# A counting sort of 50,000 edges that places the first 80 of 400 columns ahead of the other 320

## The chip, the cores and the metric

The kernel runs on one core of a Trainium2 chip. The metric is the device time of one execution in microseconds (us). A core has TensorE (PE, matrix products), VectorE (DVE, elementwise work and scans), ScalarE (ACT), GpSimd (POOL, which here writes the descriptors of indirect DMAs) and SyncE (SP, which here issues plain DMAs). They run their own instruction streams and wait for each other by semaphores.

## The reference

Four layers of a graph network on 3125 nodes of 128 features and 50,000 edges. Each layer gathers a row per edge, weighs it and sums it at the edge's target:

```python
edge_index = jnp.stack([src, dst])
h = jnp.maximum(_layernorm(x, axis=-1), 0.0)
x = x + _L0_gnn_ref(h, edge_index, edge_weight, ...)      # 3 dense layers, 2 sums over edges
h = jnp.maximum(_layernorm(x, axis=-1), 0.0)
x = x + _L1_gnn_ref(h, edge_index, edge_attr_64, ...)     # attention with 4 heads, uses edge features
h = jnp.maximum(_layernorm(x, axis=-1), 0.0)
x = x + _L2_gnn_ref(h, ..., src, dst)                     # attention with 8 heads
h = jnp.maximum(_layernorm(x, axis=-1), 0.0)
x = x + _L3_gnn_ref(h, edge_index, ...)                   # 2 gated sums over edges
```

A sum over edges is `jax.ops.segment_sum(val[:, None] * h[row], col, num_segments=N)`. The order in which the edges are summed is free, and the kernel uses that.

## The kernel before

**The sort.** Nodes are cut into 25 blocks of 128 (`NB`). Edges are sorted by the block of their target, so that later each tile of 128 edges belongs to one block and its sum is a matrix product with a one-hot matrix. The edges lie in 125 partitions (`LANES`) of 400 columns (`COLS`): `e_blk` is the block of each edge's target. Each edge has a record of 8 words (source, target within its block, weight, four edge scores) in `rec`. VectorE first counts, per partition and block, how many edges there are (line 1085), TensorE makes prefix sums of the counts over the partitions (`prefixes`, lines 775 and 776), and `base_pos[:, b]` is then the place of a partition's first edge of block b, less one.

**Placement** (lines 1103 to 1114). A loop of five rounds takes five blocks in each: five compares of `e_blk` with the block's number (`inside`, line 1105), five running sums over the columns that begin at `base_pos` (`ranks`, line 1108), and five predicated copies of the ranks to `e_pos` where the edge is in the block (line 1113), each of which waits for the one before. Lines 1116 to 1120 turn places into the rows of the DRAM table, `e_row`; line 1121 raises `s_placed`.

**Stores** (lines 442 to 452). GpSimd waits for the empty table in DRAM (`s_recinit`, filled by SyncE at line 402) and for `s_placed`, and then issues one indirect DMA for each of the 400 columns (line 449): 125 records go to the rows that `e_row` names for that column. They are in groups of 8 (`G`). Group g waits for the edge scores (`s_esc`): groups 0 to 3 for their own, all others for all 50 groups of scores; and for the stores of group g - 2 to have landed. Scores come from TensorE (transposes at line 789, products at line 799) and ScalarE (copies at lines 537 and 525), in groups of 8 columns as well, from edge features that DMAs bring in.

**Behind the stores.** SyncE waits for all stores, reads the sorted table back (line 406) and stores the node table of the first sum (lines 414 and 415). GpSimd waits for both and starts the gathers of the six sums (line 468). Meanwhile, from line 1123 on, VectorE makes tables of which tile is whose (line 1125, 25 operations), counts the edges of each node by one-hot matrices (line 1153 and 1156, multiplied by TensorE at line 822, which comes to it after the last edge product), and does the dense start of the first layer (lines 1181 to 1505). Then it waits for the sorted records (line 1269).

The order on each engine is the order of its code.

Of the kernel before, what the change touches and what calls it, by code (L numbers as in the profile page):

```python
# [8 lines left out]
ALU = mybir.AluOpType  # L9
# [3 lines left out]
P = 128  # L13
# [3 lines left out]
NB = (N + P - 1) // P  # L17
NP = NB * P
TAIL = N - (NB - 1) * P
LANES = 125  # L20
COLS = E // LANES
TILES = (E // P + NB + 15) // 16 * 16
G = 8
PAIRS = TILES // (2 * G)
GROUPS = TILES // G
SLOTS = 2 * G + 1
# [59 lines left out]
def edge_loads(eng):  # L86

    for i in range(3):
        yield i, i % 2, i // 2 + 1
    with eng.Fori(0, (COLS // 16 - 5) // 2, 1) as j:  # L90
        yield 2 * j + 3, 1, j + 2
# [21 lines left out]
def gnn_kernel(nc, x, src, dst, edge_attr, edge_weight, fc_w, fc_b, conv_w, conv_b, bn_gamma, bn_beta,  # L113
               W_node, W_edge, a_vec, Wq, bq, Wk, bk, Wv, bv, Wo, bo, Wt, bt, Wg, bg, out):
    ctx = ExitStack()
    with ctx:
# [14 lines left out]
        iota = sb("iota", [P, 512])  # L131
# [59 lines left out]
        e_w = FT[0:LANES, 2 * COLS:3 * COLS]  # L191
        e_int = FT[0:LANES, 3 * COLS:4 * COLS].bitcast(I32)
        e_blk = ACC[0:LANES, 0 * COLS:1 * COLS]
        e_sblk = ACC[0:LANES, 1 * COLS:2 * COLS]
        e_sloc = ACC[0:LANES, 2 * COLS:3 * COLS]
        e_pos = ACC[0:LANES, 3 * COLS:4 * COLS]
        e_rank = ACC[0:LANES, 4 * COLS:5 * COLS]
        row_all = ACC[:, 5 * COLS:6 * COLS].bitcast(U32)
        e_row = row_all[0:LANES, :]
        spare = sb("spare", [P, 1])  # L200
        tot = sb("tot", [LANES, NB])
        base_pos = sb("base_pos", [LANES, NB])
# [55 lines left out]
        inside = rows[0:LANES, :, :, :].rearrange("p a t f -> p (a t f)")[:, 0:5 * COLS].bitcast(I32).rearrange("p (c e) -> p c e", e=COLS)  # L258
        ranks = OH[0:LANES, :, :, :].rearrange("p a t f -> p (a t f)")[:, 0:5 * COLS].rearrange("p (c e) -> p c e", e=COLS)
# [15 lines left out]
        s_rank = sem("s_rank")  # L275
        s_masked = sem("s_masked")
        s_placed = sem("s_placed")
# [9 lines left out]
        s_esc = sem("s_esc")  # L287
# [17 lines left out]
        s_gate = sem("s_gate")  # L305
# [131 lines left out]
        @block.gpsimd  # L437
        def _(pool):
            nc.gpsimd.iota(iota_i[:, :], pattern=[[1, 512]], base=0, channel_multiplier=0).then_inc(s_iota, 1)
            nc.gpsimd.iota(lane_i[:, :], pattern=[[0, 1]], base=0, channel_multiplier=1).then_inc(s_iota, 1)  # L440

            pool.wait_ge(s_recinit, 16)
            pool.wait_ge(s_placed, 1)
            for g in range(COLS // G):
                pool.wait_ge(s_esc, g + 1 if g < 4 else COLS // G)
                if g >= 2:
                    pool.wait_ge(s_scat[(g - 2) % 3], 16 * G * ((g - 2) // 3 + 1))
                for c in range(G * g, G * g + G):
                    nc.gpsimd.indirect_dma_start(  # L449
                        rec_dram, bass.IndirectOffsetOnAxis(ap=row_all[:, c:c + 1], axis=0),  # L450
                        rec_all[:, c, :], None).then_inc(s_scat[g % 3], 16)
            pool.wait_ge(s_recl, 16)

            for k in range(len(PASSES)):
                pool.wait_ge(s_stored[k], 32)
                pool.wait_ge(s_idx, 1 if k == 0 else 2)
                idx = idx_u if k == 0 else idx_s
                for g in range(GROUPS):
                    if k in HEADS:
                        to, landed = wide[k][:, g % DEEP], s_wide[g % DEEP]  # L460
                        if g >= DEEP:
                            pool.wait_ge(s_msg, groups_before(k, ("part",)) + g - DEEP + 1)
                    else:
                        to, landed = rows[:, g % RING], s_rows[g % RING]
                        if k or g >= RING:
                            pool.wait_ge(s_part, groups_before(k, ("sum",)) + g - RING + 1)
                    for j in range(G):
                        nc.gpsimd.indirect_dma_start(  # L468
                            to[:, j, :], None, tab_dram[k],
                            bass.IndirectOffsetOnAxis(ap=idx[:, G * g + j:G * g + j + 1], axis=0)).then_inc(landed, 16)  # L470
# [551 lines left out]
        def _(dve):  # L1022
            done = [0]
            asked = [0]
            v = nc.vector

            def link(ins):
                done[0] += 1
                ins.then_inc(s_dve, 1)
                dve.wait_ge(s_dve, done[0])  # L1030
# [69 lines left out]
            link(v.memset(e_pos[:, :], 0.0))  # L1100
            link(v.memset(e_w[:, :], 0.0))

            with dve.Fori(0, NB // 5, 1) as b5:
                for c in range(5):
                    v.tensor_scalar(inside[:, c, :], e_blk[:, :], iota[0:LANES, bass.ds(5 * b5 + c, 1)], None, ALU.is_equal).then_inc(s_rank, 1)
                for c in range(5):
                    dve.wait_ge(s_rank, 15 * b5 + c + 1)
                    v.tensor_tensor_scan(ranks[:, c, :], e_w[:, :], inside[:, c, :], base_pos[:, bass.ds(5 * b5 + c, 1)],
                                         ALU.add, ALU.add).then_inc(s_rank, 1)
                for c in range(5):  # L1110
                    dve.wait_ge(s_rank, 15 * b5 + 10 + c)
                    dve.sem_inc(s_gate, 1)
                    v.copy_predicated(e_pos[:, :], inside[:, c, :], ranks[:, c, :]).then_inc(s_rank, 1)
                dve.wait_ge(s_rank, 15 * b5 + 15)

            link(v.tensor_copy(e_int[:, :], e_pos[:, :]))
            link(v.tensor_single_scalar(e_int[:, :], e_int[:, :], 7, ALU.arith_shift_right))
            link(v.tensor_copy(e_rank[:, :], e_int[:, :]))
            link(v.scalar_tensor_tensor(e_pos[:, :], e_rank[:, :], -float(P), e_pos[:, :], ALU.mult, ALU.add))
            link(v.scalar_tensor_tensor(e_row[:, :], e_pos[:, :], float(TILES), e_rank[:, :], ALU.mult, ALU.add))  # L1120
            dve.sem_inc(s_placed, 1)

            link(v.memset(tblk[:, :], 0.0))
            with dve.Fori(0, NB, 1) as b:
# [21 lines left out]
            for i in rounds(dve, COLS // G // 2):  # L1146
                for both in range(2):
                    g = 2 * i + both
                    for kind, (blk, loc) in enumerate(((e_blk[:, :], rec[:, :, R_DST]), (e_sblk[:, :], e_sloc[:, :]))):
                        buf = 2 * both + kind  # L1150
                        if there(g - 2):
                            dve.wait_ge(s_hmm, 2 * g - 3 + kind)
                        v.tensor_tensor(ohlo[:, buf * 1024:(buf + 1) * 1024].rearrange("p (g n) -> p g n", g=G),
                                        counting.unsqueeze(1).to_broadcast([LANES, G, P]),
                                        loc[:, bass.ds(G * g, G)].unsqueeze(2).to_broadcast([LANES, G, P]), ALU.is_equal).then_inc(s_rank, 1)
                        v.tensor_tensor(ohhi[:, buf, :, :], counting[:, 0:NB].unsqueeze(1).to_broadcast([LANES, G, NB]),
                                        blk[:, bass.ds(G * g, G)].unsqueeze(2).to_broadcast([LANES, G, NB]), ALU.is_equal).then_inc(s_rank, 1)
                        dve.wait_ge(s_rank, 3 * NB + 4 * g + 2 * kind + 2)
                        dve.sem_inc(s_hoh, 1)
            dve.wait_ge(s_hmm, 2 * (COLS // G))  # L1160
            for kind in range(2):
# [417 lines left out]
```

## Time and profile before

| What | Value |
|---|---|
| Median of 3 runs | 4432.37 us (4431.76 to 4432.81) |
| Profiled execution | 4432.22 us, its span 4430.4 us |
| Busy share of the span | PE 44%, VectorE 51%, ScalarE 25%, GpSimd 63% |
| GpSimd stores, line 449 | 400, 394.3 us busy, idle before them 233.4 us |
| Compares, line 1105 (125 x 400) | 25, mean 422 ns |
| Scans, line 1108 (125 x 400) | 25, mean 1027 ns |
| Predicated copies, line 1113 (125 x 400) | 25, mean 608 ns |
| Tile tables, line 1125 (128 x 416) | 25, mean 653 ns |

Times within the profile count from the start of the span. What a row calls idle is the time that an engine stood still before the instruction, with what ended it behind the arrow; "issue" means that it waited for nothing that the profile shows. An instruction's duration includes what it was held up by once it had begun.

### The profile page before, as it was taken

What the parts mean: (1) busy time and instruction counts of PE and PEld (TensorE: products, weight loads), DVE (VectorE), ACT (ScalarE), POOL (GpSimd) and SP (SyncE); (2) the same over time, 40 slices, a digit from 0 to 9 for tenths busy, and PEclk for the clock granted to TensorE, in tenths of its full rate; (3) what the DMA queues carried; (4) which work ended last, traced back from release to release, by engine and by line L of the source; (5) the groups of instructions that cost most, each with busy time, mean ns of one, the idle gap of its engine ahead of it and who ended that gap; (6) DMA issues with size and microseconds to landing.
All of it is one profiled execution on the core that took longest, in us unless ns stands there. A gap on an engine that the chain in (4) does not pass through costs nothing. (4 is left out here: it accounts for less than half of the span.)

```text
span 4430.4 us, 48122 instructions
## 1 busy us (share of the span) xinstructions
PE 1947.8 (44%) x10480; PEld 1717.4 (39%) x10507; DVE 2251.4 (51%) x5375; ACT 1094.4 (25%) x3112; POOL 2777.1 (63%) x2902
## 2 busy tenths in 40 slices
PE   7521006666433333457665445554443333433332
PEld 7411005555333333346564244544333333333332
DVE  8672027777554444346666358878523333333333
ACT  2101002222300000367775257776200000000000
POOL 0677767777467776177773077775037777177775
PEclk9997556666665556665566767777556655565555
DMA  4100012222221223133332144444011222211223
GB/s 126 37 3 3 3 38 53 53 53 52 31 57 53 52 52 48 49 76 82 79 81 31 49 129 129 129 128 85 1 38 53 53 53 52 28 52 52 53 53 51
DMA packets 145729, 254.66 MB, mean 57 GB/s; under 512 B 57658, under 2 KB 81503, under 8 KB 145300
## 3 DMA queue, kind: packets, MB, share of 16 engines
q0 software_dynamic: 99328, 193.52, 19.0%
q1 hardware_dynamic: 40058, 46.93, 3.7%
q10 hardware_dynamic: 6170, 12.57, 0.9%
q14 instruction: 145, 1.19, 0.1%
q8 instruction: 28, 0.46, 0.0%
HBM read 236.52 MB, written 16.30 MB: 57 GB/s over the span
## 5 line engine op out<-in xcount | busy, mean ns | idle before, releaser
L468 POOL DMA_INDIRECT pool<-tab_dram,tblk x1248 | 1181.8, 947 | 735.9 <-issue 379.3
L891 PE MATMUL bank<-pool 128*128 128x128 f32 x3328 | 769.6, 425 | 1522.5 <-DMA pool<-tab_dram,tblk 1037.5
L891 PEld LDWEIGHTS bank<-pool 128*128 128x128 f32 x3328 | 718.0, 327 | 1565.7 <-issue 1119.9
L468 POOL DMA_INDIRECT arena<-tab_dram,tblk x832 | 798.6, 960 | 508.0 <-DMA tab_dram<-arena 254.4
L1301 DVE TENSOR_TENSOR ACC<-ACC,bank 128x128 f32 x1664 | 476.8, 287 | 987.7 <-PE bank L891 774.5
L449 POOL DMA_INDIRECT rec_dram<-arena,ACC x400 | 394.3, 986 | 233.4 <-issue 120.1
L468 POOL DMA_INDIRECT pool<-tab_dram,arena x416 | 401.7, 966 | 141.1 <-issue 126.1
L944 PE MATMUL bank<-pool 128*128 128x136 f32 (+1 forms) x1664 | 308.6, 356 | 52.9 <-DVE pool L1374 34.2
L498 ACT ACTIVATE pool<-bank 128x512 f32<-128x512 f32 (+1 forms) x56 | 29.8, 551 | 1177.2 <-PE bank L747 1176.9
L944 PEld LDWEIGHTS bank<-pool 128*128 128x128 f32 x1664 | 292.4, 257 | 61.8 <-DVE pool L1374 37.8
L1431 DVE TENSOR_TENSOR ACC<-ACC,pool 128x132 f32 (+1 forms) x832 | 248.2, 298 | 119.2 <-DVE ACC L1431 5.8
L559 ACT ACTIVATE arena<-bank,key 128x128 bf16<-128x128 f32 x416 | 146.3, 377 | 643.8 <-PE bank L834 643.8
L618 ACT ACTIVATE pool<-iota,recS 128x128 f32<-128x128 f32 x832 | 252.8, 387 | 0.0
L920 PE MATMUL bank<-HN,pool 128*128 x832 | 155.5, 363 | 111.8 <-DVEq L1339 89.5
L920 PEld LDWEIGHTS bank<-HN,pool 128*128 128x128 f32 x832 | 143.6, 269 | 125.4 <-issue 125.4
L917 PEld LDWEIGHTS bank<-at,pool 128*128 128x128 f32 x832 | 158.9, 293 | 38.8 <-issue 38.8
L917 PE MATMUL bank<-at,pool 128*128 x832 | 158.5, 323 | 31.4 <-issue 15.7
L929 PE MATMUL bank<-ident,sg 128*128 128x128 f32 x52 | 23.1, 445 | 329.2 <-DVE lm L1363 323.2
L1197 DVE TENSOR_TENSOR pool<-bank,recS 128x1024 f32<-128x1024 f32 x104 | 127.3, 1224 | 71.4 <-issue 71.3
L1262 DVE TENSOR_SCALAR pool<-bank,arena 128x128 f32<-128x128 f32 x416 | 137.3, 401 | 39.8 <-issue 39.8
L1262 DVE TENSOR_SCALAR pool<-bank,recS 128x128 f32<-128x128 f32 x416 | 137.2, 401 | 39.9 <-issue 39.9
L929 PEld LDWEIGHTS bank<-ident,sg 128*128 128x128 f32 x52 | 9.6, 184 | 339.5 <-issue 288.9
(251 smaller groups left out, 3183.7 us busy)
## 6 DMA issues: line engine op xcount, KB each, us to landing
pool<-dst_dram SPq DMA_DIRECT2D x104, 256.0 KB, 3.5
pool<-tab_dram,tblk POOLq DMA_INDIRECT x1248
arena<-tab_dram,tblk POOLq DMA_INDIRECT x832
HN<-in_edge_attr_dram ACTq DMA_DIRECT2D x23, 500.0 KB
pool<-tab_dram,arena POOLq DMA_INDIRECT x416
rec_dram<-arena,ACC POOLq DMA_INDIRECT x400, 2.1
tab_dram<-arena SPq DMA_DIRECT2D x4, 1536.0 KB
tab_dram<-arena SPq DMA_DIRECT2D x1, 3072.0 KB
```

What stands on the lines that cost most here:

```text
L449: nc.gpsimd.indirect_dma_start(rec_dram, bass.IndirectOffsetOnAxis(ap=row_all[:, c:c + 1], axis=0), rec_all[:, c, :], None).then_inc(s_sca ...
L468: nc.gpsimd.indirect_dma_start(to[:, j, :], None, tab_dram[k], bass.IndirectOffsetOnAxis(ap=idx[:, G * g + j:G * g + j + 1], axis=0)).then ...
L559: nc.scalar.activation(signs[:, half, j, :], bank[j // 4][:, (j % 4) * P:(j % 4 + 1) * P], ACT.Sign, scale=-1.0, bias=key[:, bass.ds(G * g ...
L618: nc.scalar.activation(OHF[:, half, j, :], iota[:, 0:P], ACT.Square, scale=-1.0, bias=one[:, R_DST:R_DST + 1]).then_inc(s_osq, 1)
L891: last = nc.tensor.matmul(bank[4 + 2 * (q % 2) + j // 4][:, (j % 4) * P:(j % 4 + 1) * P], OH[:, q, j, :], rows[:, q, j, :], start=True, st ...
L917: last_ = nc.tensor.matmul(bank[4 + half][:, 4 * j:4 * j + 4], OHT[:, half, j, :], at4[:, bass.ds(vals[j], 1), :].rearrange("p b h -> p (b ...
L920: last_ = nc.tensor.matmul(bank[4 + j // 4][:, (j % 4) * P:(j % 4 + 1) * P], OHT[:, half, j, :], hn1[:, bass.ds(vals[j] * D, D)], start=Tr ...
L944: last_ = nc.tensor.matmul(bank[j // 3][:, (j % 3) * ww:(j % 3 + 1) * ww], OHF[:, half, j, :], weighed[k][:, half, j, :], start=True, stop ...
L1197: return v.tensor_tensor(to, (iota[:, 0:P] if k in HEADS else iota_p).unsqueeze(1).to_broadcast([P, G, P]), records(k)[:, bass.ds(G * g, G ...
L1262: v.tensor_scalar(OH[:, q % RING, j, :], iota_p, one[:, R_DST:R_DST + 1], one[:, R_W:R_W + 1], ALU.is_equal, ALU.mult).then_inc(s_ohw, 1)
L1301: v.tensor_tensor(acc, acc, bank[4 + 2 * (q % 2) + j // 4][:, (j % 4) * P:(j % 4 + 1) * P], ALU.add).then_inc(s_acc, 1)
L1431: v.tensor_tensor(acc, acc, own[:, j, 0:sw], ALU.add).then_inc(s_sum, 1)
```

## The change

The placement becomes a function `place(c0, c1, ranked, carry)` that works on columns c0 to c1 and is called twice, for columns 0 to 80 (`FIRST`) and 80 to 400. All instructions keep their form, with fewer columns. In the first call each round ends with a copy of the last column of `ranks` to `base_pos`, so that the second call's running sums go on from there. Each call raises `s_placed`. GpSimd begins to store after the first, with each of the first ten groups waiting for its own scores; before group 10 it waits for the second placement and for all scores. The counts on `s_rank` are moved accordingly.

```diff
+FIRST = 80
...
             for g in range(COLS // G):
-                pool.wait_ge(s_esc, g + 1 if g < 4 else COLS // G)
+                if g == FIRST // G:
+                    pool.wait_ge(s_placed, 2)
+                pool.wait_ge(s_esc, g + 1 if g < FIRST // G else COLS // G)
...
-            with dve.Fori(0, NB // 5, 1) as b5:
-                for c in range(5):
-                    v.tensor_scalar(inside[:, c, :], e_blk[:, :], iota[0:LANES, bass.ds(5 * b5 + c, 1)], None, ALU.is_equal).then_inc(s_rank, 1)
...
+            def place(c0, c1, ranked, carry):
+
+                step = 16 if carry else 15
+                with dve.Fori(0, NB // 5, 1) as b5:
+                    for c in range(5):
+                        v.tensor_scalar(inside[:, c, c0:c1], e_blk[:, c0:c1], iota[0:LANES, bass.ds(5 * b5 + c, 1)], None, ALU.is_equal).then_inc(s_rank, 1)
+                    for c in range(5):
+                        dve.wait_ge(s_rank, ranked + step * b5 + c + 1)
+                        v.tensor_tensor_scan(ranks[:, c, c0:c1], e_w[:, c0:c1], inside[:, c, c0:c1], base_pos[:, bass.ds(5 * b5 + c, 1)],
+                                             ALU.add, ALU.add).then_inc(s_rank, 1)
+                    for c in range(5):
+                        dve.wait_ge(s_rank, ranked + step * b5 + 10 + c)
+                        dve.sem_inc(s_gate, 1)
+                        v.copy_predicated(e_pos[:, c0:c1], inside[:, c, c0:c1], ranks[:, c, c0:c1]).then_inc(s_rank, 1)
+                    if carry:
+                        v.tensor_copy(base_pos[:, bass.ds(5 * b5, 5)], ranks[:, :, c1 - 1]).then_inc(s_rank, 1)
+                    dve.wait_ge(s_rank, ranked + step * b5 + step)
+
+                link(v.tensor_copy(e_int[:, c0:c1], e_pos[:, c0:c1]))
...
+                dve.sem_inc(s_placed, 1)
+
+            place(0, FIRST, 0, True)
+            place(FIRST, COLS, 16 * NB // 5, False)
```

## Rows read from the trace of the kernel before

**Rows 1.** Waits of GpSimd, 0 to 640 us: engine, line, for what, us, times, longest.

```profile
POOL rec_dram L449 <- DVEq L1121: 97.4, 1, 97.4
```

**Rows 2.** Timeline of GpSimd: start us, us, engine, line, operation, out<-in, [idle before <-releaser].

```profile
98.89 1.14 POOL L449 DMA_INDIRECT rec_dram<-arena,ACC  x1 [97.41 <-DVEq L1121]
...
139.94 0.95 POOL L449 DMA_INDIRECT rec_dram<-arena,ACC  x1 [0.30 <-issue]
155.62 0.96 POOL L449 DMA_INDIRECT rec_dram<-arena,ACC  x1 [14.72 <-ACT arena L525]
```

**Rows 3.** Timeline of all engines, 624 to 660 us.

```profile
628.20 0.96 POOL L449 DMA_INDIRECT rec_dram<-arena,ACC  x1 [0.30 <-issue]
630.34 0.35 SPq L406 DMA_DIRECT2D arena<-rec_dram  x1
...
638.39 0.53 DVE L1269 CAST arena<-arena 128x416 uint32<-128x416 f32 x1 [247.48 <-DMA arena<-rec_dram]
...
643.81 0.97 POOL L468 DMA_INDIRECT pool<-tab_dram,arena  x1 [14.65 <-DMA tab_dram<-arena]
```

**Rows 4.** Timeline of VectorE, 0 to 420 us; x5 merges five instructions.

```profile
40.04 0.21 DVE L1096 TENSOR_TENSOR_SCAN tcount<-tcount 128x25 f32<-128x25 f32 x1
...
42.24 1.78 DVE L1105 TENSOR_SCALAR pool<-ACC,iota 125x400 int32<-125x400 f32 x5 [0.26 <-DVE pool L1101]
43.93 4.81 DVE L1108 TENSOR_TENSOR_SCAN pool<-pool,base_pos 125x400 f32<-125x400 f32 x5
48.89 3.62 DVE L1113 COPY_PREDICATED ACC<-pool 125x400 f32<-125x400 int32 x5 [0.15 <-DVE pool L1108]
52.97 1.78 DVE L1105 TENSOR_SCALAR pool<-ACC,iota 125x400 int32<-125x400 f32 x5 [0.45 <-DVE ACC L1113]
...
95.58 0.37 DVE L1116 CAST pool<-ACC 125x400 int32<-125x400 f32 x1 [0.21 <-DVE ACC L1113]
...
97.40 0.58 DVE L1120 SCALAR_TENSOR_TENSOR ACC<-ACC 125x400 uint32<-125x400 f32 x1
```

**Rows 5.** Timeline of all engines, 350 to 400 us: a store beside line 1189.

```profile
351.27 3.49 DVE L1189 TENSOR_TENSOR HN<-X,stat 128x3200 f32<-128x3200 f32 x1
351.45 4.14 POOL L449 DMA_INDIRECT rec_dram<-arena,ACC  x1 [0.30 <-issue]
```

**Rows 6.** Line 402, the DMA that fills the record table: issue and landing.

```profile
L402 SPq DMA_DIRECT2D rec_dram<-recS x1: 2022/2022/2022, 25.9 to 25.9; - x1
...
DMA to landing us min/median/max: 17.1/17.1/17.1
```

**Rows 7.** Timeline of ScalarE, 20 to 60 us: the tenth copy of scores.

```profile
54.23 0.20 ACT L525 ACTIVATE arena<-bank 125x32 f32 x1 [1.00 <-PE bank L799]
```

**Rows 8.** Line 525, the copies of edge scores: duration ns, first and last start us.

```profile
L525 ACT ACTIVATE arena<-bank x50: 197/198/198, 23.3 to 155.1; 125x32 f32 x40, 125x32 f32<-125x32 f32 x10
```

**Rows 9.** Timeline of all engines, 103 to 107 us: stores beside line 1125.

```profile
104.25 0.67 DVE L1125 SCALAR_TENSOR_TENSOR tblk<-iota,tcount,tblk 128x416 f32<-128x416 f32 x1 [0.42 <-DVE tblk L1125]
104.30 0.96 POOL L449 DMA_INDIRECT rec_dram<-arena,ACC  x1 [0.30 <-issue]
...
105.34 0.65 DVE L1125 SCALAR_TENSOR_TENSOR tblk<-iota,tcount,tblk 128x416 f32<-128x416 f32 x1 [0.42 <-DVE tblk L1125]
...
105.56 1.26 POOL L449 DMA_INDIRECT rec_dram<-arena,ACC  x1 [0.30 <-issue]
```

**Rows 10.** Timeline of all engines, 1928.5 to 1931 us: a gather beside a scan.

```profile
1929.21 0.42 DVE L1351 TENSOR_TENSOR_SCAN full<-rst,fwd 128x128 f32<-128x128 f32 x1
1929.27 1.12 POOL L468 DMA_INDIRECT arena<-tab_dram,tblk  x1 [0.30 <-issue]
```

**Rows 11.** Timeline of VectorE, 130 to 175 us: the counting and its wait.

```profile
136.38 0.35 DVE L1156 TENSOR_TENSOR pool<-bank,ACC 125x200 bf16<-125x200 f32 x1
155.45 1.22 DVE L1153 TENSOR_TENSOR pool<-bank,arena 125x1024 bf16<-125x1024 f32 x1 [18.72 <-PE bank L822]
```

**Rows 12.** GpSimd's groups, 346 to 396 us: count, busy us, mean ns, idle before.

```profile
L449 POOL DMA_INDIRECT rec_dram<-arena,ACC x34 | 41.6, 1224 | 10.4 <-issue 10.1 <-DMA rec_dram<-arena,ACC 0.3
```

## What I expect of the change

> **What bounds the kernel now.** I first asked what GpSimd (POOL) waits for up to 640 us, because the 400 indirect stores of the counting sort fill that stretch [rows 1]. The longest wait is 97.4 us for VectorE's placement. Next POOL's instructions in order of time [rows 2]: the first store is at 98.89, the 32nd at 139.94, then POOL stands still for 14.72 us, until ScalarE has copied the last edge scores, and store 33 starts at 155.62. From there on 368 stores run one behind the other, to the last one at 628.20 [rows 3]: (628.20 - 155.62 - 9.0)/367 = 1.263 us each (0.96 busy and 0.30 of issue; the 9.0 are told of in part 4). Behind the last store SyncE reads the sorted records back at 630.34, VectorE wakes at 638.39 after 247.48 us of idleness, POOL gathers from 643.81 [rows 3]. So nothing but POOL's row of stores sets the time up to 640 us, and each us by which a store comes earlier is a us of the whole kernel, as long as no new wait stands in the row.
>
> The point that decides the size: what counts is not the start of the stores by itself but how many are done when store 33 used to begin. Before it was 32 at 155.62.
>
> **Part 1, the first 80 columns by themselves.** The placement runs five rounds of five blocks. One round of 400 columns takes 52.97 - 42.24 = 10.73 us: the compares 1.69, the scans up to the first predicated copy 4.96, the copies and the turn of the loop 4.08 [rows 4]. Cost per column: a scan of 25 columns takes 0.21 us [rows 4] and one of 400 columns 1.03 (the table of the profile), so (1.03 - 0.21)/375 = 2.2 ns a column. For compares and copies there is no narrow row. A copy's 0.61 us over 400 columns can't hold more than 1.5 ns a column, and a two-input operation of 3200 columns takes 3.49 us [rows 5], 1.09 ns a column with its fixed part; I take 1.04. The compare starts every 0.34 us with 400 columns, so at most 0.85 ns; I take 0.6, as estimate between nothing and that. 320 columns less save 5 x 320 x (2.2 + 1.04 + 0.6) ns = 6.1 us of a round. The carry adds one copy of five elements, bounded by nothing (hidden behind the predicated copies) and 0.2 us (the 25-column operation); I take 0.15. Five small compares can't be closer than their issue, so I add 0.2. A round: 10.73 - 6.1 + 0.35 = 5.0 us, with 4.7 to 5.4 as bounds. The loop ran from 42.24 to the first conversion at 95.58, 53.3 us; now 53.3 - 5 x 5.7 = 24.8, to 67.0. The five conversions took 2.4 (95.58 to 97.98); with 80 columns 1.3: done at 68.3. POOL started 0.9 after that before (97.98 to 98.89), so the first store is at 69.2, bounds 68 to 71. That is **29.7 us earlier**.
>
> Is anything else in the way there? The DMA that fills the record table was issued at 25.9 and landed 17.1 us later, at 43 [rows 6]. The stores of group g now wait for score g + 1 for the first ten groups; ten scores are there at 54.2 [rows 7]. No wait.
>
> **Part 2, the pause of 14.7 us.** In the old code groups 4 and up wait for all 50 score groups, which end at 155.1 [rows 8]. Now this wait stands in front of store 81. With the new start store 81 is reached at about 176, after the scores, so the pause goes: 14.7 less the ordinary 0.3 of issue, **14.4 us**. If the stores were faster than I think by 20 us it would come back; they can't be, since the issue is the bound.
>
> **Part 3, the other 320 columns while POOL stores.** A round is 10.73 - 6.1/4 = 9.2 us, five of them and conversions of 2.1: 68.6 + 45.6 + 2.1 = 116.3. POOL's new wait for it stands in front of store 81, 60 us later, so it costs nothing. What costs is that POOL and VectorE get into each other's way, which the trace shows in three places. A store that starts 0.18 us into a two-input operation of 3.49 us lasts 4.14 us instead of 0.96, up to the end of the operation [rows 5]. With the 0.65 us operations of line 1125 a store that starts 0.22 after one takes 1.26 [rows 9]. And a scan with both inputs in SBUF does it too: started 0.06 into the scan, a gather takes 1.12 instead of 0.94 [rows 10]. So a store pays what is left of the reading of the operation it falls into, and is then free. The 320-column scans read for some 0.67 us (320 columns at 2.1 ns) and come every 0.78; a store let go at the end of one starts the next 1.26 later, which is 0.37 into the second scan behind: it pays 0.29. The copies read 0.33 in 0.67, by the same phase 0.08. In a round the scans last 4.0 us (2.6 stores, 0.74 us) and the copies 3.4 (2.5 stores, 0.20). I give the compares nothing, since they are as short as 0.1 to 0.2 us. Sum 0.94 x 5 = **4.7 us**. Bounds: nothing (the predicated copy and the long scan have no row beside a store), and 22 us, if POOL doesn't get in between scans that follow each other 0.1 us apart, and every round costs a whole run of scans and the gap in front of it, 4.4 us.
>
> VectorE's side: where a store began just before or at the same time, the operation of 0.65 us took 0.67 [rows 9]. Nothing to count.
>
> The Trainium skill, page "SBUF — State Buffer", section "Who interferes with whom", says that an operation with two SBUF inputs stands in the way of a GpSimd instruction only where that one reads SBUF, and that `tensor_tensor` was not seen to stall a DMA, since descriptors need the write interface (marked there as inferred). By that rule the scans and copies would cost nothing and the sum be 4388. The 4.14 us speak against it, as the store does read its column of rows from SBUF.
>
> **Part 4, VectorE later by 18.3 us** (116.3 for 97.98). Behind the placement on its queue stand the tile tables (line 1125) and the counting of line 1153. That one already stood still: after the operation at 136.38 it waited 18.72 us for TensorE, which was still busy with the edge scores, and went on at 155.45 [rows 11]. The shift puts its first four pairs at 148.6 to 155.0, so the wait is used up and VectorE goes on within 1 us of the old time. Then it needs nothing until 638.39, and there it had 247 us to spare [rows 3]. Three operations of 3.49 us that hold a store each (the row of 351.27 and two like it) stay where they are and still hit the row of stores. Of 34 stores around them the mean is 1224 ns in place of 959 [rows 12], 34 x 0.265 = 9.0 us; the phase that they hit may change this by 2 us either way.
>
> **Sum.** 29.7 + 14.4 - 4.7 = 39.4 us. The profiled execution took 4432.22 us (span 4430.4), the median of the runs is 4432.37: 4432.3 - 39.4 = **4393**, 0.9% less. Everything behind the stores shifts as a block.
>
> **The rivals.**
> (a) No contention: scans and copies don't hold the stores. 44.1 us, 4388. Against it: [rows 5, 9, 10].
> (b) The run of scans is one hold: 22 us given back, lead 22, time 4410. For it: only 0.1 us lies between two scans. Against it: the hold in [rows 5] ended with its operation, and nothing says that a waiting store is passed over; but no row has operations that close.
> (c) The store holds VectorE for its whole 0.96 us. Then 75 operations wait up to 0.96 each, 72 us; the second placement ends at 188 and store 81 starts at 189 instead of 176: lead 27, time 4405. Against it: 0.67 instead of 0.65 [rows 9]. The same section of the Trainium skill gives this rule, whoever is first has the shared pair for the whole instruction and the other fully blocks.
> (d) Slower than before: VectorE's second placement starves. Store 81 used to start at 155.62 + 48 x 1.264 = 216.3. If the new wait lets it go later than that, the kernel is slower; for this the placement has to end after 215, take 147 us instead of 48, and each of 75 operations lose 1.3 us, more than a whole store. If each lost two stores (2.2 us) it would end at 280 and the time be 4497. What speaks for it is only that the row of stores has gaps of 0.30 us; against it again [rows 9].
> (e) The gain is not passed on: something late at 600 us beside the stores. That would be within 0.2%. Against it: the 247 us of idleness.
>
> **How the numbers follow.** My forecast 0.62; (a) 0.14; (b) 0.10; (c) 0.06; (e) 0.03; (d) 0.03; the rest, 0.02, a smaller gain of unknown cause. Time 4393. Low end: (a) with a first placement at its lower bound and 2 us of phase, 4385. High end: (b) with 1 us on it, 4411, which takes in (c). Outside lie (d), (e) and tails, under 0.15. This kernel's measurement can tell about 0.2%, 9 us, from no change. Faster by over 0.2%: all but (d) and (e), 0.94; same 0.03; slower 0.03.
>
> **What would show it.** First store at 68 to 71 us (part 1). No idle time of POOL over 1 us up to the last store, and scores no longer named as a wait (part 2). 33 to 35 stores begun before VectorE ends the second placement near 116, some of them 1.2 to 1.3 us long, none over 1.7 (part 3); stores of 3 to 4 us beside the scans would be (b), scans stretched to 1.5 us (c). VectorE's 18.7 us wait on line 822 gone and its operation behind it at 155 to 157 (part 4). Last store near 589, VectorE waking near 599. I am wrong if store 81 waits for the placement or if the idleness before line 1269 is not about 40 us shorter.

## The result and the profile after

The changed kernel takes 4395.9 us, the median of 20 runs (4389.4 to 4432.1), against 4432.9 of the kernel before in as many runs beside it: ratio 0.9936, 95% interval 0.9918 to 0.9954. The forecast was 4393. Six of the 20 runs lie at 4430.4 to 4432.1 and the other fourteen at 4389.4 to 4399.5, and the kernel before has one run in 20 at 4468.7; without these higher runs, to which the last section comes back, the medians are 4395.0 (14 runs) and 4432.8 (19 runs), 37.8 us less. The profiled execution took 4399.5 us (span 4397.7, mean granted clock 0.649), the highest of the fourteen.

The waits of GpSimd up to 640 us, as [rows 1] were: line, for what, us in total, times, longest.

```profile
POOL rec_dram L452 <- issue: 120.3, 395, 0.3
POOL rec_dram L452 <- DVEq L1129: 66.9, 1, 66.9
POOL rec_dram L452 <- ACT arena L528: 0.3, 1, 0.3
```

The placement is waited for 66.9 us in place of 97.4, and ScalarE's scores, 14.7 before, are named once with the 0.3 of an ordinary issue. The row of stores now has no hole. Its timeline (start us, us, engine, line, operation, [idle before <- what ended it]), which answers to [rows 2]:

```profile
68.34 1.14 POOL L452 DMA_INDIRECT rec_dram<-arena,ACC  x1 [66.85 <-DVEq L1129]
...
78.26 0.96 POOL L452 DMA_INDIRECT rec_dram<-arena,ACC  x1 [0.30 <-issue]
79.53 1.48 POOL L452 DMA_INDIRECT rec_dram<-arena,ACC  x1 [0.30 <-issue]
81.32 1.25 POOL L452 DMA_INDIRECT rec_dram<-arena,ACC  x1 [0.30 <-issue]
82.87 1.17 POOL L452 DMA_INDIRECT rec_dram<-arena,ACC  x1 [0.30 <-DMA rec_dram<-arena,ACC]
84.34 1.03 POOL L452 DMA_INDIRECT rec_dram<-arena,ACC  x1 [0.30 <-issue]
...
588.50 0.96 POOL L452 DMA_INDIRECT rec_dram<-arena,ACC  x1 [0.30 <-issue]
```

The first store starts 30.6 us earlier (98.89 before), the last one 39.7 us earlier (628.20 before). VectorE's timeline, from the first round of the first placement to the end of the counting's wait ([rows 4] and [rows 11] before):

```profile
42.28 0.94 DVE L1111 TENSOR_SCALAR pool<-ACC,iota 125x80 int32<-125x80 f32 x5 [0.26 <-DVE pool L1104]
43.15 1.48 DVE L1114 TENSOR_TENSOR_SCAN pool<-pool,base_pos 125x80 f32<-125x80 f32 x5
44.78 1.84 DVE L1119 COPY_PREDICATED ACC<-pool 125x80 f32<-125x80 int32 x5 [0.15 <-DVE pool L1114]
46.52 0.16 DVE L1121 COPY base_pos<-pool 125x5 f32 x1
47.13 0.94 DVE L1111 TENSOR_SCALAR pool<-ACC,iota 125x80 int32<-125x80 f32 x5 [0.45 <-DVE base_pos L1121]
...
78.59 3.98 DVE L1114 TENSOR_TENSOR_SCAN pool<-pool,base_pos 125x320 f32<-125x320 f32 x5
82.71 3.19 DVE L1119 COPY_PREDICATED ACC<-pool 125x320 f32<-125x320 int32 x5
...
115.88 0.49 DVE L1128 SCALAR_TENSOR_TENSOR ACC<-ACC 125x320 uint32<-125x320 f32 x1
...
156.03 1.23 DVE L1164 TENSOR_TENSOR pool<-bank,arena 125x1024 bf16<-125x1024 f32 x1 [0.88 <-PE bank L825]
```

A round of 80 columns takes 47.13 - 42.28 = 4.85 us, the second placement is done at 116.37, and the wait of 18.72 us behind it has shrunk to 0.88, with the operation that it held at 156.03 (155.45 before). The stores of 79.53 to 84.34 in the fence above are some of the ones held: they fall beside the scans of 78.59 and the predicated copies of 82.71. At the far end of the sort, the timeline of all engines ([rows 3] before):

```profile
590.64 0.35 SPq L407 DMA_DIRECT2D arena<-rec_dram  x1
...
598.62 0.53 DVE L1280 CAST arena<-arena 128x416 uint32<-128x416 f32 x1 [207.35 <-DMA arena<-rec_dram]
...
603.93 0.98 POOL L471 DMA_INDIRECT pool<-tab_dram,arena  x1 [14.48 <-DMA tab_dram<-arena]
```

VectorE's idleness is 207.35 us in place of 247.48, 40.1 less: it pays for the lead with time that it had to spare, and the first gather starts 39.9 us earlier.

### The profile page after: what moved, and what is told of

The parts are those of the page before. It is cut to its first block and busy times, and to the rows that moved or that the text cites. A ratio compares the mean times of both kernels' runs of the same rounds, so it can differ in the third digit from the quotient of the medians.

```text
span 4397.7 us, 48349 instructions
## 1 busy us (share of the span) xinstructions
PE 1958.4 (45%) x10480; PEld 1729.4 (39%) x10507; DVE 2266.0 (52%) x5460; ACT 1094.4 (25%) x3112; POOL 2786.0 (63%) x2902
## 5 line engine op out<-in xcount | busy, mean ns | idle before, releaser
L932 PE MATMUL bank<-ident,sg 128*128 128x128 f32 x52 | 22.8, 439 | 325.4 <-DVE lm L1374 319.0
L1273 DVE TENSOR_SCALAR pool<-bank,recS 128x128 f32<-128x128 f32 x416 | 137.9, 402 | 40.2 <-issue 40.1
L1273 DVE TENSOR_SCALAR pool<-bank,arena 128x128 f32<-128x128 f32 x416 | 137.3, 402 | 39.7 <-issue 39.6
```

The lines of the kernel that those rows point to most:

```text
L1273: v.tensor_scalar(OH[:, q % RING, j, :], iota_p, one[:, R_DST:R_DST + 1], one[:, R_W:R_W + 1], ALU.is_equal, ALU.mult).then_inc(s_ohw, 1)
```

## Experiments

The theory: the row of stores sets the end of the sort; its gain is the earlier start (29.7) plus the score wait that the new rule passes over (14.4), less what VectorE's operations with SBUF inputs take from the stores. The rivals to be told apart: that one of the two edits does all of it; that the holds don't come from the inputs in SBUF; and the ones of the forecast. The first four kernels were run together with the kernel before and fell into a condition in which every kernel, the one before too, took some 5450 us. They can't decide the sizes, so all four were run again.

**The changed kernel again, 5450 us.** No edit.

> The changed kernel as it stands, to see how far its runs scatter. Theory (the store row is the clock of the first 600 us, everything behind it shifts as a block): first store at 68.3 us, last store at 588.5, first gather at 603.9, time near 4395. Of the 20 runs of it so far 7 lay at 4430 to 4432 and 13 at 4389 to 4400, of the kernel before one in 20 lay 36 us above the rest. Theory A of that: a step of some 36 us behind the sort that both kernels can take, not tied to the stores; then a profile of a high run has its last store at 588.5 too and is longer later on. Theory B: in the high runs the gain of the sort itself is lost, and the last store is at 625.

(The list of the 20 runs has six at 4430 to 4432, not seven; this count stands in the later expectations too.)

Measured: 5448.3 us (5427.8 to 5483.2, 12 runs) against 5463.3 of the kernel before (35 runs), ratio 0.9971 [0.9952, 0.9990]. VectorE's timeline shows what the condition is, and below it the late scores, in the timeline of all engines:

```profile
156.10 0.65 DVE L1136 SCALAR_TENSOR_TENSOR tblk<-iota,tcount,tblk 128x416 f32<-128x416 f32 x1 [4.96 <-issue]
...
171.00 0.20 ACT L528 ACTIVATE arena<-bank 125x32 f32 x1 [20.90 <-issue]
...
237.68 0.20 ACT L528 ACTIVATE arena<-bank 125x32 f32<-125x32 f32 x1 [1.48 <-PE bank L802]
237.98 1.23 DVE L1164 TENSOR_TENSOR pool<-bank,arena 125x1024 bf16<-125x1024 f32 x1 [36.49 <-PE bank L825]
238.62 0.95 POOL L452 DMA_INDIRECT rec_dram<-arena,ACC  x1 [62.67 <-issue]
```

The operations themselves keep their length (0.65 us), but 4.96 us lie between two of them where the loop took 0.42 at 119 us of the same trace, and the profile names nothing waited for but the issue. ScalarE stood still for 20.9 us in the same way. Up to 97 us nothing of this is seen in this trace: the first store is at 68.3, as in the first result. Then the last scores come at 237.7, some 80 us late, and the pause that the change had passed over is back in front of store 81, 62.7 us long. So the gain depends on the scores being there when store 81 is due; here, where they came 60 us after that, 15 us of it were left. The kernel before has no profile in this condition, so where its own pause lay isn't known. Why the engines issued so slowly isn't settled either; the last section says when they did.

**The split alone,** with the old rule for the scores:

```
-                pool.wait_ge(s_esc, g + 1 if g < FIRST // G else COLS // G)
+                pool.wait_ge(s_esc, g + 1 if g < 4 else COLS // G)
```

Under the 5450 us condition:

> Placement split as in the change, but stores of groups 4 and up wait for all edge scores again. Theory (the gain is the number of stores done at 155.6, so part 1 alone is worth nothing): first store at 68.3, 32 stores by 113, then a pause of about 43 us until 155.4, last store at 628, time 4432, ratio 1.000. Rival (each part is worth its own share): 30 less 5 of holds, last store at 603, time 4408, ratio 0.994.

Measured: 5452.9 us, ratio 0.9975 [0.9960, 0.9990]; a pause of 66.7 us in front of store 33, which starts at 180.5, and the last store at 668.5. The sign of the pause is as forecast, but with scores this late (the last copy at 179.99) the size says nothing of the ordinary case. Again, without the condition:

> The split alone once more, since in the first look the engines' own sequencers stalled (VectorE, ScalarE and TensorE stood still for up to 21 us at a time with nothing to wait for, in every kernel, the one before included) and the whole took 5450 us. Theory, without those stalls: first store at 68.3, store 33 at 155.6 behind a pause of about 43 us, last store at 628, ratio 1.000. Rival (each part is worth its own share): last store at 603, ratio 0.994.

(Of the kernel before, only the time is known in that condition, 5463.3 us; that its engines stood still in the same way wasn't seen.)

Measured: 4436.6 us (4432.9 to 4473.8, 10 runs) against 4434.0, ratio 1.0014 [0.9996, 1.0032]. GpSimd's waits, and the store behind the pause:

```profile
POOL rec_dram L452 <- DVEq L1129: 66.8, 1, 66.8
POOL rec_dram L452 <- ACT arena L528: 42.0, 2, 41.7
```

```profile
155.76 0.96 POOL L452 DMA_INDIRECT rec_dram<-arena,ACC  x1 [41.69 <-ACT arena L528]
...
627.34 0.96 POOL L452 DMA_INDIRECT rec_dram<-arena,ACC  x1 [0.31 <-issue]
```

The first store came at 68.24, as in the changed kernel, and 32 were done; then POOL stood for 41.7 us and store 33 started at 155.76, where it started before (155.62). Of the 30.7 us by which the stores began earlier, 27.0 became a longer wait (41.7 for 14.7) and the rest went into stores held beside the placement. The split by itself gains nothing.

**The score rule alone,** in the kernel before:

```
-                pool.wait_ge(s_esc, g + 1 if g < 4 else COLS // G)
+                pool.wait_ge(s_esc, g + 1 if g < 10 else COLS // G)
```

Under the 5450 us condition:

> Placement in one piece as in the kernel before; only the rule for the scores is that of the change (the first ten groups wait for their own). Theory: first store at 98.9, no pause, last store at 628.2 - 14.4 = 613.8, time 4418, ratio 0.9968. Rival (the early stores hinder the loading of the edge features and so the scores): scores end later than 155.1, and store 81 waits for them, gain under 10 us.

Measured: 5463.7 us, ratio 0.9992 [0.9979, 1.0006]; store 81 waited 49 us, until 250.4. No gain: the pause stood in front of store 81, and the scores that ended it came at 249.90, 70 us later than in the split alone. In this condition it is the rival of the expectation that was seen, early stores with late scores. Again, without the condition:

> The scores' rule alone once more (the first look stood under the sequencers' stalls). Theory: no pause at store 33, last store at 613.8, time 14.4 us under the kernel before, ratio 0.9968. Rival (early stores hinder the edge features): gain under 10 us. With the split alone at 1.0014, theory says that the two parts give 0 and 14.4 us apart and 39.7 together.

Measured: 4422.6 us (4416.5 to 4425.2, 12 runs) against 4436.4, ratio 0.9958 [0.9939, 0.9977]. GpSimd's timeline:

```profile
99.33 1.14 POOL L449 DMA_INDIRECT rec_dram<-arena,ACC  x1 [97.85 <-ACT arena L525]
...
613.47 0.96 POOL L449 DMA_INDIRECT rec_dram<-arena,ACC  x1 [0.30 <-issue]
...
629.03 0.97 POOL L468 DMA_INDIRECT pool<-tab_dram,arena  x1 [14.61 <-DMA tab_dram<-arena]
```

The last store is 14.7 us earlier than before (628.20), the median 13.8. The last scores were copied at 156.60 (155.1 before), so the rival isn't seen here. So of the 39.7 us at the last store the split alone brings 0.9, the score rule alone 14.7, and the other 24 are there only with both.

**The changed kernel a third time,** beside the variants that follow and the score rule alone:

> The changed kernel once more. Theory (the store row is the clock of the first 600 us, what is behind it shifts as a block): last store at 588.5 us, ratio 0.991 in the runs of the lower level. 7 of its 20 first runs lay 36 us higher, at the time of the kernel before, and of the kernel before 1 of 20 lay 36 us above its own level. Theory A: both kernels have a second level 36 us above the first, by something behind the sort; a profile of a high run has its last store at 588.5. Theory B: the high runs lose the gain of the sort, last store at 625.

Measured: 4398.6 us (9 runs, 7 of them at 4395.4 to 4399.6 with a median of 4398.1) against 4436.4, ratio 0.9921 [0.9888, 0.9954]. First store 68.09, last 587.68; its stores beside the placement again lost 5.7 us. What the first result showed repeats itself to within 1 us.

**The scans' zeros in PSUM.** The scan adds a row of zeros to the row of hits; the zeros were an SBUF tile and are now a PSUM bank, so that one of the two long inputs no longer comes out of SBUF:

```
-            link(v.memset(e_w[:, :], 0.0))
+            zeros = bank[5][0:LANES, 0:COLS]
+            link(v.memset(zeros, 0.0))
...
-                        v.tensor_tensor_scan(ranks[:, c, c0:c1], e_w[:, c0:c1], inside[:, c, c0:c1], ...
+                        v.tensor_tensor_scan(ranks[:, c, c0:c1], zeros[:, c0:c1], inside[:, c, c0:c1], ...
```

Under the 5450 us condition:

> As the changed kernel, but the zeros that are the scans' first input lie in PSUM, so a scan has one input in SBUF. Theory (two inputs in SBUF hold the stores, 4.3 us of the 5.7 us that 34 stores lose up to 117 us are lost beside scans): stores beside scans take 0.96, last store at 584.2, time about 4 us under the changed kernel's. Rival (VectorE's work as such slows the stores, or the predicated copies and compares do it): the 1.25 us stores stay and the last store is at 588.5.

Measured: 5458.2 us, ratio 0.9987 [0.9973, 1.0000]; its store 81 waited 81.5 us for the scores, which hides whatever the stores gain ahead of it. Again, without the condition:

> Zeros of the scans in PSUM, once more. Theory (two inputs in SBUF hold the stores; 4.3 of the 5.7 us that are lost up to 117 us are lost beside scans): stores beside scans take 0.96 us, last store at 584.2, about 4 us under the changed kernel. Rival (VectorE's work as such slows the stores): the stores of 1.25 us stay, last store at 588.5.

Measured: 4393.5 us (4391.8 to 4397.0, 6 runs) against 4436.4, ratio 0.9889 [0.9854, 0.9923]. GpSimd's row at the place where the changed kernel had stores of 1.48, 1.25 and 1.17 us:

```profile
78.72 0.96 POOL L452 DMA_INDIRECT rec_dram<-arena,ACC  x1 [0.30 <-issue]
79.99 0.96 POOL L452 DMA_INDIRECT rec_dram<-arena,ACC  x1 [0.30 <-issue]
81.25 0.96 POOL L452 DMA_INDIRECT rec_dram<-arena,ACC  x1 [0.30 <-issue]
82.51 0.96 POOL L452 DMA_INDIRECT rec_dram<-arena,ACC  x1 [0.31 <-issue]
```

and VectorE's beside it:

```profile
78.46 3.97 DVE L1115 TENSOR_TENSOR_SCAN pool<-bank,base_pos,pool 125x320 f32<-125x320 f32 x5
82.58 3.19 DVE L1120 COPY_PREDICATED ACC<-pool 125x320 f32<-125x320 int32 x5
```

Five scans take 3.97 us beside them and 3.98 in the changed kernel: the scan costs the same, only the store beside it is free. Grouped by line from 68 to 117 us (count, busy us, mean ns), the changed kernel has

```profile
L452 POOL DMA_INDIRECT rec_dram<-arena,ACC x34 | 38.3, 1128 | 76.9 <-DVEq L1129 66.9 <-issue 9.8 <-DMA rec_dram<-arena,ACC 0.3
```

and the one with the zeros in PSUM

```profile
L452 POOL DMA_INDIRECT rec_dram<-arena,ACC x39 | 38.2, 980 | 78.2 <-ACT arena L528 66.7 <-issue 11.3 <-DMA rec_dram<-arena,ACC 0.3
```

Against 0.96 us each, that is 34 x 0.168 = 5.7 us lost in the one and 39 x 0.020 = 0.8 in the other. The last store is at 583.85, 3.8 us earlier than in the third run of the changed kernel. So the holds are real, and beside the scans it takes both inputs in SBUF. The predicated copies weren't changed: that the store of 82.51 is free where the changed kernel had 1.17 is a matter of phase, and eight other stores beside copies still lost 0.5 us together (up to 1.11 us long). The time is 4.6 us under the seven lower runs of the changed kernel beside it, for the 4 forecast.

**The first 40 columns by themselves,** with the score rule for the first 12 groups:

```
-FIRST = 80
+FIRST = 40
+SCORED = 12
...
-                pool.wait_ge(s_esc, g + 1 if g < FIRST // G else COLS // G)
+                pool.wait_ge(s_esc, g + 1 if g < SCORED else COLS // G)
```

> As the changed kernel with 40 columns first in place of 80, and the first 12 groups of stores waiting for their own scores (so that store 41 waits for the second placement alone). A round of the first placement takes 4.85 us with 80 columns, 10.73 with 400: 18 ns a column, so 5 rounds of 40 columns less save 3.7 us. Theory: first store at 64.5, second placement done at 116.5, store 41 due at 121, no wait, last store at 585.2, 3.3 us under the changed kernel. Rival (the placement of 360 columns, held up by the stores, is not done when store 41 is due): a wait of some us before store 41 and no gain.

Measured: 4394.4 us (4393.9 to 4397.1, 6 runs), ratio 0.9889 [0.9855, 0.9924]. First store 64.66, no wait in front of store 41, last store 586.17. The start came 3.4 us earlier, as forecast, but the last store only 1.5: the second placement is now 360 columns wide, and the stores beside it lost 6.9 us against 5.7, and another 1.2 at the long operations of 345 to 400 us (8.7 against 7.5). Here the theory had the start right and the holds too small. The median is 3.7 us under the seven lower runs of the changed kernel, near the 3.3 forecast, but by luck: the sort gave 1.5 of them, and the rest lies behind it, where single executions scatter by as much.

**Both together,** 40 columns and the zeros in PSUM:

> 40 columns first, the first 12 groups on their own scores, and the scans' zeros in PSUM: both gains together. Theory (40 columns first start the stores 3.4 us earlier; PSUM zeros take away most of what the stores lose beside scans, 7 us of it with 360 columns): first store at 64.7, no wait before store 41 (due at 117, the second placement done at 116; if it is late, by under 2 us), last store at 580.5, time 7 us under the changed kernel. Rival (without the holds store 41 is due before the second placement is done): a wait of over 3 us before store 41, last store at 584 as with 80 columns.

Measured under the 5450 us condition again: 5462.3 us (5454.3 to 5495.3, 11 runs) against 5472.9, ratio 0.9992 [0.9976, 1.0009]. POOL waited twice, and the first wait was for the second placement and not for scores:

```profile
143.98 0.96 POOL L453 DMA_INDIRECT rec_dram<-arena,ACC  x1 [28.00 <-DVEq L1131]
...
263.06 0.96 POOL L453 DMA_INDIRECT rec_dram<-arena,ACC  x1 [47.75 <-ACT arena L529]
```

The placement ended at 143.6 in place of 116.5, as VectorE too issued slowly from 83 us on, and the last scores came at 262.8. So the run says nothing of the ordinary case, nor of the rival. Whether the two gains add up stays open.

**Two single executions of the changed kernel,** for the 36 us between the two levels:

> The changed kernel, one look, in the hope of a profile of the level 36 us higher (9 of 29 runs so far lay there, 3 of 53 of the kernel before). Theory A (something behind the sort): last store at 588, and one of the six gather passes longer by 36. Theory B: last store at 625. A run of the lower level shows neither.

> As the look before it, for the same question. Theory A: last store at 588 and one later stage 36 us longer. Theory B: last store at 625. A run of the lower level shows neither.

Measured: 5455.0 and 5501.5 us, the 5450 us condition in both, 46.5 us apart. What they show stands in the last section.

## Why the prediction was right, and where it was off

**What bounds the kernel.** Right. The row of stores was followed to 588.50, and the first gather moved by the same 39.9 us as the last store (39.7). Nothing late turned up beside it: rival (e) is out.

**The step that decides the size,** that only the stores done by the time store 33 used to begin count, and not the earlier start: shown by the split alone, whose 32 stores were done earlier, and whose store 33 began no earlier (155.76 for 155.62).

**Part 1.** First store at 68.3 for 69.2 (68 to 71). The round of 80 columns took 4.85 for 5.0. From the widths 80 and 320 the costs per column come out as taken: five scans 1.48 and 3.98 us at 80 and 320 columns, 2.50/(5 x 240) = 2.1 ns a column for 2.2; five predicated copies 1.84 and 3.19, 1.1 for 1.04. The columns' bounds from distant rows held.

**Part 2.** 14.4 forecast, 14.7 by the rule alone. Right, with the qualification of the 5450 us runs: it rests on the scores being done before store 81 is due, at about 177. They were there at 156 and had some 20 us to spare.

**Part 3.** The second placement was done at 116.37 for 116.3, 34 stores had begun, and none took over 1.48 (forecast: none over 1.7). The term that was mis-sized is the holds: 5.7 us in place of 4.7. Read store by store, 4.3 us of them lie beside the scans (forecast 3.7), 1.2 beside the predicated copies (forecast 1.0), and the last 0.2 are the first store's, which took 1.14 us in the kernel before as well. The number of stores was right (13 beside scans for 5 x 2.6, 12 beside copies for 5 x 2.5), and so was the phase of a row that runs: a store that began 0.37 to 0.39 us into a scan took 1.24 to 1.25, 0.29 of it held. What the forecast left out is the first store beside each run of scans, which from the second round on began 0.14 to 0.26 us into a scan and was held for 0.52 or 0.41. The compares cost nothing, as taken, but the reason given (as short as 0.1 to 0.2 us) is wrong: they take 404 ns on average at 320 columns. And the store of [rows 5] did not end with the operation of 3.49 us, it ended 0.83 us behind it (355.59 for 354.76); what ended with the operation is the hold. The cause was named rightly: take the zeros out of SBUF, and 0.8 us are left. With that rival (a), no contention, is out for this kernel; near it comes only the PSUM variant, whose last store was 44.4 us before that of the kernel before, where (a) had said 44.1. Rival (b), a run of scans as one hold, is out: no store took over 1.48, so POOL does get in between two scans that start 0.78 us apart. Rivals (c) and (d) are out: the scans kept their length (859 ns each on average in the changed kernel, 856 with the zeros in PSUM, where none holds a store), though 21 of the 25 began while a store was running.

The Trainium skill, page "SBUF — State Buffer", section "Who interferes with whom", says that an operation with two SBUF inputs contends only with GpSimd instructions that read SBUF, and infers that it doesn't stall a DMA, because descriptors need the write interface. By that rule the time would have been the 4388 of rival (a). The first half agrees with the PSUM variant (1.48 to 0.96 us); the inference doesn't hold for these indirect stores, which the scans hold for up to 0.52 us. The same section's rule that whoever comes first blocks the other for the whole instruction doesn't hold here either: the stores, 0.96 us long, left the scans beside them at their length.

**Part 4.** VectorE's operation behind the wait at 156.03 (155 to 157). Right. Last store 588.50 for 589, VectorE awake at 598.62 for 599.

**Sum.** 39.4 forecast, 39.7 at the last store. Against the forecast the start is 0.9 us better, the holds beside the placement 1.0 worse, those behind it up to 146 us 0.3 worse (2.2 for the 1.9 that the first 32 stores lost before, which the forecast took as unchanged), the three long operations 1.3 better (7.7 for 9.0), and some 0.6 is spread over the other stores, 2 ns on each. What didn't hold exactly is the sentence that everything behind the stores shifts as a block. The table gives the starts of the six passes of gathers, in us:

| pass | before | after | difference |
|---|---|---|---|
| 1 | 643.81 | 603.93 | -39.9 |
| 2 | 1238.39 | 1200.13 | -38.3 |
| 3 | 1856.72 | 1821.22 | -35.5 |
| 4 | 2539.73 | 2505.66 | -34.1 |
| 5 | 3273.52 | 3239.05 | -34.5 |
| 6 | 3876.82 | 3843.46 | -33.4 |
| end of the span | 4430.4 | 4397.7 | -32.7 |

Seven microseconds seep away in small steps. Whether they are a second effect of the change isn't shown: from the first gather to the end of the span it was 3786.6 us before, 3793.8 and 3794.2 in two profiles of the changed kernel, 3790.5 with the zeros in PSUM, 3792.1 with 40 columns, 3785.7 with the score rule alone and 3790.9 with the split alone. The two profiles without the split are the shortest, but each is one execution, and runs of one kernel scatter by up to 10 us, more than the loss. The medians say 37.8, so about 2 us of the 39.7 may be lost behind the sort.

**The range and the chances.** The median lies well inside. But six single runs lie at 4430 to 4432, above the high end of 4411. My rivals were all about the sort; a level of the run that is set 1800 us behind it wasn't among them. It was to be seen neither in the profile of before nor in its three times.

## What to carry to other kernels

Two edits that open the same row have to be costed together: 0.9 and 14.7 us alone became 39.7, and the way to see it is to ask which instruction the next wait stands in front of and when it was due before. A row of GpSimd's DMAs ran on beside VectorE's short operations at 1.43 us each in place of 1.26; putting a constant operand into PSUM took most of that away at no cost to VectorE. Where the lead is made of waits that are passed over, ask how late the input may come before the wait is back: here 20 us, and in the 5450 us runs it came some 60 us later than that.

## What the runs showed of the hardware that I had not expected

**A second level 36 us up.** The runs of a kernel fall into two groups: of the changed kernel 8 of 29 lie 35 to 37 us above the rest, of the kernel before 3 of 53 (36 to 38 us), of the split alone 1 of 10, of the other variants none of 24 (all without the 5450 us condition). The two single executions of the changed kernel, 5455.0 and 5501.5 us, differ by 46.5. Five us of that lie in the sort (last stores 660.11 and 665.07), some six in the passes between, and 35 in the wait ahead of the fourth pass of gathers. GpSimd's timeline at the start of that pass, in the shorter one:

```profile
3197.89 0.95 POOL L471 DMA_INDIRECT arena<-tab_dram,tblk  x1 [180.67 <-DMA tab_dram<-arena]
```

in the longer one:

```profile
3244.02 0.94 POOL L471 DMA_INDIRECT arena<-tab_dram,tblk  x1 [215.65 <-DMA tab_dram<-arena]
```

What the gathers wait for is made by TensorE, 50 products of 128x384 and their 50 biases. TensorE's groups by line (count, busy us, mean ns) in the shorter one:

```profile
L1008 PE MATMUL bank<-wT,pool 128*128 128x384 f32 x50 | 22.8, 538 | 0.6 <-ACT pool L501 0.6
L1009 PE MATMUL bank<-brow,ones 1*128 1x384 f32 x50 | 22.7, 533 | 0.0
```

in the longer one:

```profile
L1009 PE MATMUL bank<-brow,ones 1*128 1x384 f32 x50 | 40.4, 907 | 0.0
L1008 PE MATMUL bank<-wT,pool 128*128 128x384 f32 x50 | 40.3, 909 | 0.4 <-ACT pool L501 0.4
```

The profiles of the kernel before and of the changed kernel, both of the lower level, agree with the shorter one (22.7 us at line 1006 and 1009, 533 ns each). 40.3 + 40.4 - 22.8 - 22.7 = 35.2 us, about the distance of the levels. TensorE's timeline of the longer one shows where it turns:

```profile
3151.20 0.91 PE L1008 MATMUL bank<-wT,pool 128*128 128x384 f32 x2 [0.37 <-ACT pool L501]
3152.04 0.91 PE L1009 MATMUL bank<-brow,ones 1*128 1x384 f32 x2
3152.88 1.48 PE L1008 MATMUL bank<-wT,pool 128*128 128x384 f32 x2
3154.29 1.64 PE L1009 MATMUL bank<-brow,ones 1*128 1x384 f32 x2
3155.86 1.65 PE L1008 MATMUL bank<-wT,pool 128*128 128x384 f32 x2
```

For 3154 to 3198 us of it this is the row of a table by stretches (busy us of TensorE, its weight load, VectorE, ScalarE, GpSimd; granted clock; DMA share; GB/s):

```profile
3154.00:3198.00 44.00, 44.00 (x57) 13.98 (x56) 0.00 (x0) 9.28 (x28) 0.00 (x0) 0.50 0.00 0
```

The granted clock is 0.50, the 1.2 GHz level, while TensorE is busy all the time. Ahead of the products it had stood still for 49.3 us and done 25 transposes, and the first two products and the first two biases still took 0.91 us for two. In the shorter execution it had stood still for 49.0 us ahead of the same 25 transposes, and the pairs stay at 0.91 us, the clock at 0.99, through the stage (3141 to 3185 us). So what these rows show of the engine ahead of the products doesn't tell the two apart. Both kernels have runs 36 us above their others, so it isn't the change that makes the level. Why the changed kernel takes the higher one more often (8 of 29 against 3 of 53) is open; that the high runs without the 5450 us condition have the same cause is argued from the same 36 us alone, as none of them was profiled.

**Stretches of slow issue.** Twice every kernel of a group that was run together took about 1030 us longer (5463 and 5473 against 4433 to 4436 for the kernel before). The packets and bytes of DMA were the same and TensorE's and VectorE's busy time within 5% (2028 and 2270 us in the changed kernel, 1948 and 2251 in the kernel before without the condition), but 2 to over 20 us lay between instructions with nothing waited for. GpSimd's stores alone kept their 1.26 us from one to the next up to some 440 us.

The traces show one thing more, which bears on the gain: in the sort the slow issue goes with the stores. In the changed kernel VectorE's waits of over 1.5 us with nothing waited for lie at 121 to 182 us; POOL stored until 176 and then stood still until 239. In the split alone POOL stood still from 114 to 180, and there VectorE's tile tables, with up to 4.96 us between two of them in the trace above, ran through at their ordinary pace:

```profile
131.82 0.65 DVE L1136 SCALAR_TENSOR_TENSOR tblk<-iota,tcount,tblk 128x416 f32<-128x416 f32 x1 [0.42 <-DVE tblk L1136]
```

The last scores came at 180 with 32 stores ahead of them, and at 238 to 263 in the six traces in which 80 or 96 stores went ahead. In none of the seven traces does such a wait of VectorE begin more than 5 us after POOL has stopped, until POOL stores again. These rows suggest that in this condition the stores slow the issue, and that storing early makes the scores late; no experiment was made for it, and what brings the condition about is open. A gain read in it is another one: 15 us in place of 38.

**A store held by an operation with SBUF inputs** lost at most 0.52 us here beside the scans (1.48 in place of 0.96), never more than what was left of one scan, while the scan kept its length.
